# A decoder layer on one core: softmax normalised on POOL ahead of the transposes, in place of the spread and transposed reciprocals

## The chip, the cores and the metric

One core of a Trainium2 chip runs one program. The metric is the device time of an execution in microseconds; lower is better. Three runs of the kernel before took 1832.89, 1834.21 and 1837.18 us, median 1834.21.

## What is computed

32 sequences of 128 tokens, 512 wide, pass one decoder layer in fp32. Cut to what matters:

```python
x = x + attn(layernorm(x))              # 16 heads of 32, rotary, causal
x = x + xattn(layernorm(x), ctx)        # 32 heads of 16, axial rotary, ctx 128 x 256
x = x + ffn(layernorm(x))               # gate, up: 512 -> 1408, silu, down: 1408 -> 512
# both attentions, per head:
w = softmax(scores, axis=-1)            # rows: queries, columns: keys
ctx = w @ v                             # then @ Wo
```

The softmax is exp(s - max) divided by its row sum. The division can be made on the 128x128 probabilities of each head, or on the 32 or 16 output columns of that head.

## The kernel before

The program has two phases. The attention phase treats one sequence (128 tokens, one per partition) after the other; the FFN phase treats blocks of four sequences and is not touched by the change. Each engine has its own instruction stream, written out by hand in the function `turn` of its block, and streams wait for each other by semaphores. Nothing but the code's order sets the order of work.

A turn of the attention phase is a software pipeline over sequences. `turn(sq, cq, nx, nz, oq)` does for sequence sq its self-attention (unit "1": 16 heads), for cq = sq - 1 its cross attention in two halves ("2a" and "2b", 16 heads each), for nx the projections q1, k1, v1, for nz the first layernorm, and for oq = sq - 2 the last half of its cross attention and the output projection o2. The loop (`schedule`) has 27 such turns in a hardware loop and some more unrolled before and after it.

Each unit goes through the same steps with four PSUM banks S[0] to S[3], four heads to a bank:
- TensorE makes the scores (`scores1`, `scores2`) in all four banks.
- DVE takes the negated row maxima, a bank at a time (`row_maxima`, L831).
- ACT takes the exponentials into `prob` in SBUF, a head at a time, with the row sums accumulated (`exponentials`, L650).
- TensorE transposes the 16 heads' probabilities back into the same banks, a bank when it is ready (`transpose_prob`, through `transpose4`, L443).
- ACT copies banks 1 and 3 and DVE banks 0 and 2 to `probT` (`odd_copies` L657, `even_copies` L837). `collect` makes TensorE wait for all four before it writes the next scores into the banks.
- TensorE multiplies by v (`attend1` L497 into bank PC, `attend2` L507 into bank PB); the outcome is transposed: features on partitions.

While ACT takes exponentials, TensorE projects (`project`, L456: three passes over a high and a low part, since the fp32r operands hold less than fp32). The rotary embedding is made by DVE as two products (`rope`, L785 and L788), summed by POOL (`rope_sum`, L382), and transposed by TensorE.

The normalisation lies behind the attention. DVE takes the reciprocals of the row sums (L878 for unit 1, L937 for both halves of unit 2). POOL spreads each over its head's columns (`spread`, L388, to `rbc`, 128x512), TensorE transposes the spread tile by four transposes into bank TC, ACT copies it to SBUF (`rT1` L680, `rT2` L667), and DVE multiplies the attention's output by it twice, once rounded to `cn_h` and once in full to `cn` (`normalise_ctx`, L822 and L823). POOL takes `cn_l = cn - cn_h` (`ctx_low`, L401), and o1 and o2 are projected from the two parts.

The two layernorms share the pattern of `statistics` (DVE), `rough_rstd` (POOL, L378) and `normalise` (DVE: three small steps of one column, L768 to L771, then z, L773). POOL's stream also has `split_ctx` (L394, L397) and the sum x1B (L419). The rest of DVE's work in a turn: the residual sums x2 (L872) and x1A (L898), the reduction of a window of the FFN weights (L913), kT2 (L921, L922), kT1 (L928) and the low parts of z1T and z2T (L826).

Of the kernel before, what the change touches and what calls it, by code (L numbers as in the profile page):

```python
# [138 lines left out]
def attention_phase(nc, fp32, fp32r, ALU, ACT, AX, x, ctx_in, pos, consts,  # L139
                    wq1, wk1, wv1, wo1, wq2, wkv2, wo2, bout, x2_dram, shared_f, shared, ident, mhalf_c, ffn):  # L140
    es = ExitStack()
    with es:
# [42 lines left out]
        rsum1, rsum2 = sb("rsum1", [P, H1]), sb("rsum2", [P, H2])  # L185
        rinv1, rinv2 = sb("rinv1", [P, H1]), sb("rinv2", [P, H2])
        rbc1, rbc2 = sb("rbc1", [P, H1, DK1]), sb("rbc2", [P, H2, DK2])
        rT1, rT2 = sb("rT1", [P, D]), sb("rT2", [P, D])

        cn, cn_h, cn_l = sb("cn", [P, KT, P]), sb("cn_h", [P, KT, P], fp32r), sb("cn_l", [P, KT, P], fp32r)  # L190
# [13 lines left out]
        turns_sb, pos_sb = rT2[:, 0:B * 2 * HALF], rT2[:, B * 2 * HALF:B * 2 * HALF + 2 * B]  # L204
# [41 lines left out]
        rb_r = {n: sem(f"rinv{n}_spread") for n in (1, 2)}  # L246
        ri_d = {n: sem(f"rinv{n}T_done") for n in (1, 2)}
        riT_r = {n: sem(f"rinv{n}T_ready") for n in (1, 2)}
        cn_r = {n: sem(f"ctxn{n}_ready") for n in (1, 2)}
# [109 lines left out]
        def _(pool):  # L359
# [952 lines left out]
```

## Time and profile before

| | us |
|---|---|
| runs (3) | 1832.89 to 1837.18, median 1834.21 |
| profiled execution | 1831.93 |
| its span, first to last instruction | 1830.1 |
| busy: TensorE / DVE / ACT / POOL | 1699.3 / 1157.3 / 964.0 / 480.7 |
| mean granted TensorE clock | 0.977 |

The span is what the trace covers; the execution takes 1.8 us more. Each page and answer is of this one execution. A busy time is the sum of an engine's records; a group is all instructions of one line, operation and shape. The idle time before an instruction is given with what ended it. A line of `transpose4` or `project` is a helper's, so one tells its uses by the operands: `bank<-ident,prob` transposes probabilities, `bank<-ident,rbc` the spread reciprocals.

### The profile page before, as it was taken

Reading aid. Unit: us, or ns where it says so; the run is one execution under the profiler, and the core shown is the slowest. Engines: PE = TensorE matmul, PEld = TensorE weight load, DVE = VectorE, ACT = ScalarE, POOL = GpSimd, SP = SyncE. Lnnn points to the kernel's source line nnn. Section 1 sums busy time; section 2 is a strip of 40 time slices with the busy share of each in tenths; the row PEclk is TensorE's granted clock in tenths of the full one; section 3 lists DMA queues with packets and bytes.
Section 4 is the critical chain, followed back from the end, with each engine's and each line's share of the span. In section 5 each row is a group of like instructions: output and inputs, shape, how many; then the busy total and the mean of one; then the engine's idle time right before and its main releaser. Section 6 shows DMA issues by size and latency. Waiting matters only on the chain. (4 is left out here: it accounts for less than half of the span.)

```text
span 1830.1 us, 36507 instructions
## 1 busy us (share of the span) xinstructions
PE 1699.3 (93%) x12736; PEld 1376.3 (75%) x12736; DVE 1157.3 (63%) x2143; ACT 964.0 (53%) x3791; POOL 480.7 (26%) x470
## 2 busy tenths in 40 slices
PE   3799999999999999999999999997699999999997
PEld 2577777777777777777777777775478888888885
DVE  4677777777777777777777777765464343443432
ACT  4366666666666666666666666665342222222221
POOL 1233333333333333333333333332001110110111
PEclk8899999999999999999999999998699999999999
DMA  5010111001110011100101001020511101110110
GB/s 194 15 32 19 43 34 33 28 28 45 32 33 28 28 46 31 33 28 28 46 31 33 28 28 46 19 78 7 179 36 70 69 0 69 69 50 18 69 46 23
DMA packets 55095, 80.95 MB, mean 44 GB/s; under 512 B 4880, under 2 KB 25488, under 8 KB 55056
## 3 DMA queue, kind: packets, MB, share of 16 engines
q1 hardware_dynamic: 55056, 80.43, 13.5%
q8 instruction: 25, 0.41, 0.1%
q14 instruction: 14, 0.11, 0.0%
HBM read 63.63 MB, written 16.78 MB: 44 GB/s over the span
## 5 line engine op out<-in xcount | busy, mean ns | idle before, releaser
L650 ACT ACTIVATE prob<-bank,nmax 128x128 f32<-128x128 f32 x1536 | 537.4, 406 | 107.4 <-DVE nmax L831 107.4
L650 ACT ACTIVATION_READ_ACCUMULATOR prob<-bank,nmax 128x1 f32 x1536 | 378.4, 246 | 0.0
L831 DVE TENSOR_REDUCE nmax<-bank 128x4 f32<-128x512 f32 x384 | 240.9, 682 | 96.3 <-PE bank L478 71.0
L1107 PE MATMUL fbank<-shared,piece_hi 128*128 128x512 f32 x1152 | 280.3, 394 | 0.0
L1107 PEld LDWEIGHTS fbank<-shared,piece_hi 128*128 128x128 f32 x1152 | 215.8, 187 | 53.2
L382 POOL TENSOR_TENSOR rope_buf<-rope_buf 128x512 f32<-128x512 f32 x128 | 165.5, 1293 | 299.8 <-DVE rope_buf L788 299.4
L456 PE MATMUL bank<-shared,z1T_h 128*128 128x512 f32 x768 | 204.5, 409 | 5.1 <-DVE shared L945 3.8
L1259 DVE SCALAR_TENSOR_TENSOR h<-fbank,su_c,sil 128x512 f32<-128x512 f32 x88 | 66.0, 750 | 218.3 <-PE fbank L1107 218.2
L443 PE MATMUL bank<-ident,prob 128*128 128x128 f32 x1536 | 191.4, 277 | 11.0 <-ACT prob L650 11.0
L443 PEld LDWEIGHTS bank<-ident,prob 128*128 128x128 f32 x1536 | 174.4, 143 | 20.6 <-ACT prob L650 16.6
L657 ACT ACTIVATE probT<-bank 128x512 f32<-128x512 f32 x192 | 115.3, 600 | 130.4 <-PE bank L443 130.4
L456 PEld LDWEIGHTS bank<-shared,z1T_h 128*128 128x128 f32 x768 | 142.4, 192 | 47.4 <-issue 16.4
L1193 ACT ACTIVATE sil<-fbank,sg_c 128x512 f32<-128x512 f32 x88 | 60.4, 687 | 172.7 <-PE fbank L1107 171.9
L1199 ACT ACTIVATE h_h<-h 128x512 fp32r<-128x512 f32 x88 | 55.6, 632 | 177.1 <-DVE h L1259 177.1
L837 DVE COPY probT<-bank 128x512 f32<-128x512 f32 x192 | 126.3, 683 | 16.7 <-PE bank L443 14.8
L401 POOL TENSOR_TENSOR cn_l<-cn,cn_h 128x512 fp32r<-128x512 f32 x64 | 82.5, 1289 | 185.7 <-DVE cn L823 185.7
L388 POOL TENSOR_TENSOR rbc<-rinv,one_c 128x512 f32<-128x512 f32 x64 | 66.5, 1038 | 233.7 <-DVE rinv L937 182.3
L1122 PE MATMUL fbank<-piece_hi,h_h 128*128 128x512 f32 x288 | 115.3, 400 | 0.6 <-DVE h_l L1262 0.5
L1090 POOL TENSOR_TENSOR xr<-xr,ys 128x512 f32<-128x512 f32 x32 | 40.2, 1289 | 288.0 <-DVE ys L1279 288.0
L1122 PE MATMUL fbank<-piece_hi,h_l 128*128 128x512 f32 x288 | 113.6, 394 | 0.0
L456 PE MATMUL bank<-shared,z1T_l 128*128 128x512 f32 x384 | 105.0, 395 | 0.0
L1262 DVE TENSOR_TENSOR h_l<-h,h_h 128x512 fp32r<-128x512 f32 x88 | 62.8, 713 | 61.4 <-ACT h_h L1199 61.4
(156 smaller groups left out, 2925.7 us busy)
## 6 DMA issues: line engine op xcount, KB each, us to landing
xA<-in_x SPq DMA_DIRECT2D x32, 256.0 KB, 2.8
xB<-in_x SPq DMA_DIRECT2D x32, 256.0 KB, 2.8
x_scratch<-x SPq DMA_DIRECT2D x32, 256.0 KB, 2.0
shared_loaded<-x_scratch SPq DMA_DIRECT2D x8, 1024.0 KB, 7.7
xr<-x_scratch SPq DMA_DIRECT2D x8, 1024.0 KB, 5.6
out<-xr SPq DMA_DIRECT2D x8, 1024.0 KB, 4.3
cx<-in_ctx SPq DMA_DIRECT2D x32, 128.0 KB, 2.2
range_window<-in_wg SPq DMA_DIRECT2D x27, 112.0 KB, 2.0
```

The source lines that it names most:

```text
L382: pool.tensor_tensor(RA[n][:, :], RA[n][:, :], RB[n][:, :], ALU.add).then_inc(rot[n], 1)
L388: pool.tensor_tensor(tile[:, :, :], r[:, :].unsqueeze(2).to_broadcast([P, h, w]), one_c[:, :].unsqueeze(2).to_broadcast([P, h, w]), ALU.mu ...
L401: pool.tensor_tensor(cn_l[:, :, :], cn[:, :, :], cn_h[:, :, :], ALU.subtract).then_inc(cn_lo[n], 1)
L443: last = nc.tensor.transpose(dst[:, j * P:(j + 1) * P], src(j), ident[:, :])
L456: last = nc.tensor.matmul(dst[:, :], a[:, j, :], w[:, j, cols], start=(n == 0), stop=(n == 3 * k - 1))
L650: last = nc.scalar.activation(prob[:, c, i, :], S[c][:, i * P:(i + 1) * P], ACT.Exp, bias=nmax[:, c, i:i + 1], accum_out=rs[:, h:h + 1])
L657: nc.scalar.activation(probT[:, c, :, :].rearrange("p g t -> p (g t)"), S[c][:, :], ACT.Copy).then_inc(pTo_r[kind(u)], 1)
L831: nc.vector.tensor_reduce(out=nmax[:, c, :], in_=S[c][:, :].rearrange("p (g k) -> p g k", g=G), op=ALU.max, axis=AX, negate=True).then_inc ...
L837: nc.vector.tensor_copy(probT[:, c, :, :].rearrange("p g t -> p (g t)"), S[c][:, :]).then_inc(pTe_r[kind(u)], 1)
L1107: last = nc.tensor.matmul(dst[:, :], w[:, k, cols], z[:, k, :], start=(n == 0), stop=(n == len(passes) * KT - 1))
L1122: last = nc.tensor.matmul(DN[s][:, :], a[j % 2][:, tok], w[piece][:, j % 2, :], start=(j == 0 and n == 0), stop=(j == HT - 1 and n == len( ...
L1259: nc.vector.scalar_tensor_tensor(out=h[j % 2][:, :], in0=UP[j % 2][:, :], scalar=su_c[:, j:j + 1], in1=sil[j % 2][:, :], op0=ALU.mult, op1 ...
```

## The change

The probabilities are divided by their row sums before they are transposed.
- DVE takes reciprocals of two banks' sums at a time (`reciprocals`, six of 8 columns a turn), each when the exponentials of these two banks are done.
- POOL multiplies `prob` in SBUF, in place, a bank at a time, by the reciprocals broadcast over 128 keys (`normalise_prob`): 12 products of 128x512 a turn, in pairs.
- `transpose_prob` waits for these products (semaphore `prob1_normalised` or `prob2_normalised`) where it waited for the exponentials.
- `spread`, the transposes of `rbc`, the copies rT1 and rT2, the products `normalise_ctx` and POOL's `ctx_low` go, with their tiles and semaphores. ACT rounds the attention's output to `cn_h` (`ctx_high`, behind the exponentials of the next unit's bank 0), DVE takes `cn_l` from PSUM (`ctx_low`), and o1 and o2 wait for cn_l at their start.
- The transposes of 2b's banks 2 and 3 stand behind those of k1 and z1, and their copies accordingly.

Row sums and reciprocals share one tile for all units. The start-up scratch of the rotary tables moves from rT2 to x2.

```diff
@@ -182,12 +182,8 @@
 nmax = sb("nmax", [P, G, G])
-rsum1, rsum2 = sb("rsum1", [P, H1]), sb("rsum2", [P, H2])
-rinv1, rinv2 = sb("rinv1", [P, H1]), sb("rinv2", [P, H2])
-rbc1, rbc2 = sb("rbc1", [P, H1, DK1]), sb("rbc2", [P, H2, DK2])
-rT1, rT2 = sb("rT1", [P, D]), sb("rT2", [P, D])
-cn, cn_h, cn_l = sb("cn", [P, KT, P]), sb("cn_h", [P, KT, P], fp32r), sb("cn_l", [P, KT, P], fp32r)
+rsum, rinv = sb("rsum", [P, G, G]), sb("rinv", [P, G, G])
+cn_h, cn_l = sb("cn_h", [P, KT, P], fp32r), sb("cn_l", [P, KT, P], fp32r)
@@ -381,12 +374,12 @@
-def spread(n, q, r, tile, h, w):
-    wait(pool, ri_d[n], q)
-    pool.wait_ge(ri_r[n], q + 1)
-    pool.tensor_tensor(tile[:, :, :], r[:, :].unsqueeze(2).to_broadcast([P, h, w]),
-                       one_c[:, :].unsqueeze(2).to_broadcast([P, h, w]), ALU.mult).then_inc(rb_r[n], 1)
+def normalise_prob(u, q, half):
+    pool.wait_ge(ri_r[kind(u)], 2 * nth(u, q) + half + 1)
+    for c in (2 * half, 2 * half + 1):
+        pool.tensor_tensor(prob[:, c, :, :], prob[:, c, :, :], rinv[:, c, :].unsqueeze(2).to_broadcast([P, G, P]),
+                           ALU.mult).then_inc(pn_r[kind(u)], 1)
@@ -396,13 +389,9 @@
-def ctx_low(n, q):
-    pool.wait_ge(cn_r[n], q + 1)
-    pool.tensor_tensor(cn_l[:, :, :], cn[:, :, :], cn_h[:, :, :], ALU.subtract).then_inc(cn_lo[n], 1)
 def turn(sq, cq, nx, nz, oq):
-    if oq is not None:
-        ctx_low(2, oq)
+    if sq is not None:
+        normalise_prob("1", sq, 0)
@@ -411,25 +400,29 @@
     if sq is not None:
-        spread(1, sq, rinv1, rbc1, H1, DK1)
+        normalise_prob("1", sq, 1)
...
-    if sq is not None:
-        ctx_low(1, sq)
+    if cq is not None:
+        normalise_prob("2a", cq, 0)
     if nx is not None:
         rope_sum("q1", nx)
+    if cq is not None:
+        normalise_prob("2a", cq, 1)
...
+    if cq is not None:
+        normalise_prob("2b", cq, 0)
...
     if cq is not None:
-        spread(2, cq, rinv2, rbc2, H2, DK2)
+        normalise_prob("2b", cq, 1)
@@ -480,9 +473,9 @@
-def transpose_prob(u, q):
-    for c in range(G):
-        pe.wait_ge(p_r[kind(u)], G * nth(u, q) + c + 1)
+def transpose_prob(u, q, banks=range(G)):
+    for c in banks:
+        pe.wait_ge(pn_r[kind(u)], G * nth(u, q) + c + 1)
@@ -528,30 +521,19 @@
     if has_o:
-        pe.wait_ge(rb_r[2], oq + 1)
-        if has_c:
-            pe.wait_ge(zT_hi[2], cq + 1)
-            pe.wait_ge(zT_lo[2], cq + 1)
-        transpose4(TC, columns(rbc2[:, :, :].rearrange("p h d -> p (h d)"))).then_inc(ri_d[2], 1)
...
     if has_o:
-        pe.wait_ge(cn_r[2], oq + 1)
-        project(PB, cn_h, cn_l, "o2", KT, lo_ready=(cn_lo[2], oq + 1), fresh=is_first(oq)).then_inc(pj["o2"], 1)
-    if has_c:
-        if has_o:
-            pe.wait_ge(riT_r[2], oq + 1)
+        pe.wait_ge(cn_lo[2], oq + 1)
+        project(PB, cn_h, cn_l, "o2", KT, fresh=is_first(oq)).then_inc(pj["o2"], 1)
+    if has_c:
...
         transpose_prob("1", sq)
-        pe.wait_ge(rb_r[1], sq + 1)
-        if has_c:
-            pe.wait_ge(v2_r, cq + 1)
-        transpose4(TC, columns(rbc1[:, :, :].rearrange("p h d -> p (h d)"))).then_inc(ri_d[1], 1)
@@ -570,10 +552,11 @@
         pe.wait_ge(cxT_lo, sq + 1)
-        pe.wait_ge(riT_r[1], sq + 1)
+        if has_c:
+            pe.wait_ge(v2_r, cq + 1)
         project(TC, cxT_h, cxT_l, "kv2", CKT, slice(0, D), fresh=is_first(sq)).then_inc(pj["k2"], 1)
-        pe.wait_ge(cn_r[1], sq + 1)
-        project(PC, cn_h, cn_l, "o1", KT, lo_ready=(cn_lo[1], sq + 1), fresh=is_first(sq)).then_inc(pj["o1"], 1)
+        pe.wait_ge(cn_lo[1], sq + 1)
+        project(PC, cn_h, cn_l, "o1", KT, fresh=is_first(sq)).then_inc(pj["o1"], 1)
@@ -597,13 +580,15 @@
     if has_c:
-        transpose_prob("2b", cq)
+        transpose_prob("2b", cq, (0, 1))
...
         transpose_z1(nz)
+    if has_c:
+        transpose_prob("2b", cq, (2, 3))
@@ -639,20 +624,20 @@
-def exponentials(u, q):
-    rs = (rsum1, rsum2)[kind(u) - 1]
-    if u != "2b":
-        wait(act, ri_r[kind(u)], q)
-    for c in range(G):
+def exponentials(u, q, banks=range(G)):
+    for c in banks:
         act.wait_ge(nmax_r[kind(u)], G * nth(u, q) + c + 1)
         for i in range(G):
-            h = head(u, c, i)
             last = nc.scalar.activation(prob[:, c, i, :], S[c][:, i * P:(i + 1) * P], ACT.Exp,
-                                        bias=nmax[:, c, i:i + 1], accum_out=rs[:, h:h + 1])
+                                        bias=nmax[:, c, i:i + 1], accum_out=rsum[:, c, i:i + 1])
         last.then_inc(p_r[kind(u)], 1)
-def odd_copies(u, q):
-    for c in (1, 3):
+def ctx_high(n, q, src):
+    act.wait_ge(av_d[n], (q + 1) * n)
+    nc.scalar.activation(flat(cn_h), src[:, :], ACT.Copy).then_inc(cn_hi[n], 1)
+def odd_copies(u, q, banks=(1, 3)):
+    for c in banks:
@@ -662,11 +647,12 @@
             nc.scalar.activation(ffn["zT_h"][:, k, :], FZ[k][:, :], ACT.Copy).then_inc(f_zTh, 1)
+    if has_s:
+        exponentials("1", sq, (0,))
     if has_o:
-        act.wait_ge(ri_d[2], oq + 1)
-        nc.scalar.activation(rT2[:, :], TC[:, :], ACT.Copy).then_inc(riT_r[2], 1)
-    if has_s:
-        exponentials("1", sq)
+        ctx_high(2, oq, PB)
+    if has_s:
+        exponentials("1", sq, (1, 2, 3))
@@ -676,11 +662,13 @@
         odd_copies("1", sq)
-        act.wait_ge(ri_d[1], sq + 1)
-        nc.scalar.activation(rT1[:, :], TC[:, :], ACT.Copy).then_inc(riT_r[1], 1)
-    if has_c:
-        exponentials("2a", cq)
+    if has_c:
+        exponentials("2a", cq, (0,))
+    if has_s:
+        ctx_high(1, sq, PC)
+    if has_c:
+        exponentials("2a", cq, (1, 2, 3))
@@ -692,9 +680,11 @@
     if has_c:
-        odd_copies("2b", cq)
+        odd_copies("2b", cq, (1,))
     if nz is not None:
         z1T_high(nz)
+    if has_c:
+        odd_copies("2b", cq, (3,))
@@ -817,11 +807,6 @@
-def normalise_ctx(n, src, r):
-    nc.vector.tensor_tensor(flat(cn_h), src[:, :], r[:, :], ALU.mult).then_inc(cn_hi[n], 1)
-    nc.vector.tensor_tensor(flat(cn), src[:, :], r[:, :], ALU.mult).then_inc(cn_r[n], 1)
@@ -831,8 +816,17 @@
-def even_copies(u, q):
-    for c in (0, 2):
+def reciprocals(u, q, half):
+    c = slice(2 * half, 2 * half + 2)
+    dve.wait_ge(p_r[kind(u)], G * nth(u, q) + 2 * half + 2)
+    nc.vector.reciprocal(rinv[:, c, :], rsum[:, c, :]).then_inc(ri_r[kind(u)], 1)
+def ctx_low(n, q, src):
+    dve.wait_ge(cn_hi[n], q + 1)
+    low(cn_l, src[:, :], cn_h, cn_lo[n])
+def even_copies(u, q, banks=(0, 2)):
+    for c in banks:
@@ -855,9 +849,9 @@
     if has_o:
-        dve.wait_ge(riT_r[2], oq + 1)
-        dve.wait_ge(av_d[2], 2 * oq + 2)
-        normalise_ctx(2, PB, rT2)
+        ctx_low(2, oq, PB)
+    if has_s:
+        reciprocals("1", sq, 0)
@@ -865,6 +859,8 @@
         statistics(1, xA, nz)
+    if has_s:
+        reciprocals("1", sq, 1)
@@ -873,25 +869,23 @@
     if has_s:
-        dve.wait_ge(p_r[1], G * (sq + 1))
-        wait(dve, rb_r[1], sq)
-        nc.vector.reciprocal(rinv1[:, :], rsum1[:, :]).then_inc(ri_r[1], 1)
...
     if has_c:
-        row_maxima("2a", cq, (0, 1))
-    if has_s:
-        dve.wait_ge(riT_r[1], sq + 1)
-        dve.wait_ge(av_d[1], sq + 1)
-        normalise_ctx(1, PC, rT1)
-    if has_c:
-        row_maxima("2a", cq, (2, 3))
+        row_maxima("2a", cq, range(G))
+    if has_s:
+        ctx_low(1, sq, PC)
+    if has_c:
+        reciprocals("2a", cq, 0)
...
         rope("k2", sq, TC, DK2, *axial(sq), 1.0)
+    if has_c:
+        reciprocals("2a", cq, 1)
+    if has_s:
@@ -914,27 +908,29 @@
         ffn_normalise()
+    if has_c:
+        reciprocals("2b", cq, 0)
     if has_n:
         rope("k1", nx, PA, DK1, cos1, sin1, 1.0)
+    if has_c:
+        reciprocals("2b", cq, 1)
...
     if has_c:
-        even_copies("2b", cq)
+        even_copies("2b", cq, (0,))
...
         z1T_low(nz)
+    if has_c:
+        even_copies("2b", cq, (2,))
...
         low(z2T_l, TC[:, :], z2T_h, zT_lo[2])
-    if has_c:
-        dve.wait_ge(p_r[2], 2 * G * (cq + 1))
-        wait(dve, rb_r[2], cq)
-        nc.vector.reciprocal(rinv2[:, :], rsum2[:, :]).then_inc(ri_r[2], 1)
```

POOL's stream, first half of a turn (the unrolled one ahead of the loop; the loop's are alike). Before:

```order
L401 TENSOR_TENSOR cn_l<-cn,cn_h 128x512 [waits ctxn2_ready]
L382 TENSOR_TENSOR rope_buf<-rope_buf 128x512 [waits rope_q2_products]
L378 TENSOR_TENSOR r<-ve,mhalf 128x1 [waits var_eps1_ready]
L388 TENSOR_TENSOR rbc<-rinv,one_c 128x512 [waits rinv1_ready,rinv1T_done]
L394 TENSOR_TENSOR cxT_h<-cx,one_c 128x256 [waits proj_v2_done,ctx_loaded]
L397 TENSOR_TENSOR cxT_l<-cx,cxT_h 128x256 [waits ctxT_hi_ready]
L419 TENSOR_TENSOR x1B<-x1A,bout_b 128x512 [waits x2_ready,x1_ready]
```

The same stretch of the change:

```order
L381 TENSOR_TENSOR prob<-prob,rinv 128x512 [waits rinv1_ready]
L381 TENSOR_TENSOR prob<-prob,rinv 128x512
L375 TENSOR_TENSOR rope_buf<-rope_buf 128x512 [waits rope_q2_products]
L371 TENSOR_TENSOR r<-ve,mhalf 128x1 [waits var_eps1_ready]
L381 TENSOR_TENSOR prob<-prob,rinv 128x512 [waits rinv1_ready]
L381 TENSOR_TENSOR prob<-prob,rinv 128x512
L387 TENSOR_TENSOR cxT_h<-cx,one_c 128x256 [waits proj_v2_done,ctx_loaded]
L390 TENSOR_TENSOR cxT_l<-cx,cxT_h 128x256 [waits ctxT_hi_ready]
L408 TENSOR_TENSOR x1B<-x1A,bout_b 128x512 [waits x2_ready,x1_ready]
```

Two products stand ahead of rope q2 and the rough rstd, and two behind them. The second half of POOL's turn, before:

```order
L401 TENSOR_TENSOR cn_l<-cn,cn_h 128x512 [waits ctxn1_ready]
L382 TENSOR_TENSOR rope_buf<-rope_buf 128x512 [waits rope_q1_products]
L382 TENSOR_TENSOR rope_buf<-rope_buf 128x512 [waits rope_k2_products]
L378 TENSOR_TENSOR r<-ve,mhalf 128x1 [waits var_eps2_ready]
L382 TENSOR_TENSOR rope_buf<-rope_buf 128x512 [waits rope_k1_products]
L388 TENSOR_TENSOR rbc<-rinv,one_c 128x512 [waits rinv2_ready,rinv2T_done]
```

The same stretch of the change:

```order
L381 TENSOR_TENSOR prob<-prob,rinv 128x512 [waits rinv2_ready]
L381 TENSOR_TENSOR prob<-prob,rinv 128x512
L375 TENSOR_TENSOR rope_buf<-rope_buf 128x512 [waits rope_q1_products]
L381 TENSOR_TENSOR prob<-prob,rinv 128x512 [waits rinv2_ready]
L381 TENSOR_TENSOR prob<-prob,rinv 128x512
L375 TENSOR_TENSOR rope_buf<-rope_buf 128x512 [waits rope_k2_products]
L371 TENSOR_TENSOR r<-ve,mhalf 128x1 [waits var_eps2_ready]
L381 TENSOR_TENSOR prob<-prob,rinv 128x512 [waits rinv2_ready]
L381 TENSOR_TENSOR prob<-prob,rinv 128x512
L375 TENSOR_TENSOR rope_buf<-rope_buf 128x512 [waits rope_k1_products]
L381 TENSOR_TENSOR prob<-prob,rinv 128x512 [waits rinv2_ready]
L381 TENSOR_TENSOR prob<-prob,rinv 128x512
```

Each of the cross attention's halves has a rotary sum between its two pairs of products. On TensorE the end of a turn moves too (z is a layernorm's output). Before:

```order
L443 MATMUL bank<-ident,prob 128x128 [waits prob2_ready]
L443 MATMUL bank<-ident,prob 128x128 x3
L443 MATMUL bank<-ident,rope_buf 128x128 [waits rope_k1_ready]
L443 MATMUL bank<-ident,rope_buf 128x128 x3
L443 MATMUL bank<-ident,z 128x128 [waits z1_ready,v1_ready]
L443 MATMUL bank<-ident,z 128x128 x3
L443 MATMUL bank<-ident,z 128x128 [waits k2T_ready,z2_ready]
```

In the change:

```order
L436 MATMUL bank<-ident,rope_buf 128x128 [waits rope_k1_ready]
L436 MATMUL bank<-ident,rope_buf 128x128 x3
L436 MATMUL bank<-ident,z 128x128 [waits z1_ready,v1_ready]
L436 MATMUL bank<-ident,z 128x128 x3
L436 MATMUL bank<-ident,prob 128x128 [waits prob2_normalised]
L436 MATMUL bank<-ident,prob 128x128 x3
L436 MATMUL bank<-ident,prob 128x128 [waits prob2_normalised]
L436 MATMUL bank<-ident,prob 128x128 x3
L436 MATMUL bank<-ident,z 128x128 [waits k2T_ready,z2_ready]
```

The last two banks of 2b come behind k1 and z1, ahead of z2.

## Rows read from the trace of the kernel before

**Rows 1.** The page: busy us, share of the span and instructions of each engine
```profile
PE 1699.3 (93%) x12736; PEld 1376.3 (75%) x12736; DVE 1157.3 (63%) x2143; ACT 964.0 (53%) x3791; POOL 480.7 (26%) x470
```
**Rows 2.** Timeline of TensorE over one turn: start, duration, line, operation, [idle before <-releaser]
```profile
649.82 1.02 PE L463 MATMUL bank<-causal,ident_b 128*128 128x512 bf16 x4 [0.33 <-DVE kT L928]
...
652.69 0.63 PE L443 MATMUL bank<-ident,rbc 128*128 128x128 f32 x4 [0.75 <-POOL rbc L388]
...
661.73 1.91 PE L443 MATMUL bank<-ident,prob 128*128 128x128 f32 x16
...
664.38 1.15 PE L478 MATMUL bank<-kT,qT 32*128 32x256 f32 x16 [0.30 <-issue]
...
673.48 1.91 PE L443 MATMUL bank<-ident,prob 128*128 128x128 f32 x16
...
676.17 1.15 PE L478 MATMUL bank<-kT,qT 32*128 32x256 f32 x16 [0.34 <-ACT probT L657]
...
687.93 1.02 PE L463 MATMUL bank<-causal,ident_b 128*128 128x512 bf16 x4 [0.33 <-DVE kT L928]
```
**Rows 3.** TensorE's longest wait; scores1's first matmuls from 100 us on; the turn as a stretch
```profile
PE bank L443 <- POOL rbc L388: 28.5, 32, 3.6
L463 PE MATMUL bank<-causal,ident_b x120: 376/377/379, 116.5 to 1222.0; 128*128 128x512 bf16 x120
649.82:687.93 38.11, 36.40 (x329) 29.75 (x330) 28.37 (x55) 24.95 (x112) 13.42 (x13) 1.00 0.11 33
```
**Rows 4.** Timeline of POOL, DVE and ACT in the same turn
```profile
651.41 1.04 POOL L388 TENSOR_TENSOR rbc<-rinv,one_c 128x512 f32<-128x512 f32 x1 [5.24 <-DVE rinv L937]
652.01 2.48 DVE L831 TENSOR_REDUCE nmax<-bank 128x4 f32<-128x512 f32 x4 [0.75 <-PE bank L468]
658.85 1.29 POOL L382 TENSOR_TENSOR rope_buf<-rope_buf 128x512 f32<-128x512 f32 x1 [1.78 <-DVE rope_buf L788]
659.74 0.15 DVE L762 TENSOR_SCALAR ve<-mv 128x1 f32<-128x1 f32 x1
660.79 0.21 DVE L768 SCALAR_TENSOR_TENSOR nt<-r,ve 128x1 f32<-128x1 f32 x1
661.51 0.55 DVE L773 TENSOR_SCALAR z<-xA,mv,nt 128x512 f32<-128x512 f32 x1
661.97 0.25 DVE L878 RECIPROCAL rinv<-rsum 128x16 f32<-128x16 f32 x1
666.66 0.36 ACT L650 ACTIVATE prob<-bank,nmax 128x128 f32<-128x128 f32 x1
667.00 0.37 ACT L650 ACTIVATE prob<-bank,nmax 128x128 f32<-128x128 f32 x1
```
**Rows 5.** POOL's groups of the whole trace: count, busy us, mean ns of one, idle before
```profile
L382 POOL TENSOR_TENSOR rope_buf<-rope_buf 128x512 f32<-128x512 f32 x128 | 165.5, 1293 | 299.8 <-DVE rope_buf L788 299.4
L388 POOL TENSOR_TENSOR rbc<-rinv,one_c 128x512 f32<-128x512 f32 x64 | 66.5, 1038 | 233.7 <-DVE rinv L937 182.3 <-DVE rinv L878 51.4
L397 POOL TENSOR_TENSOR cxT_l<-cx,cxT_h 128x256 fp32r<-128x256 f32 x32 | 23.2, 726 | 2.5
L394 POOL TENSOR_TENSOR cxT_h<-cx,one_c 128x256 fp32r<-128x256 f32 x32 | 19.6, 613 | 0.7 <-DMA cx<-in_ctx 0.7
```
**Rows 6.** DVE beneath POOL in the FFN: timeline, and that line's ns (min/median/max)
```profile
1379.86 5.04 POOL L1090 TENSOR_TENSOR xr<-xr,ys 128x512 f32<-128x512 f32 x4 [30.11 <-DVE ys L1279]
1384.49 0.96 DVE L1262 TENSOR_TENSOR h_l<-h,h_h 128x512 fp32r<-128x512 f32 x1 [0.70 <-ACT h_h L1199]
L1262 DVE TENSOR_TENSOR h_l<-h,h_h x88: 691/691/975, 1320.8 to 1816.7; 128x512 fp32r<-128x512 f32 x88
```
**Rows 7.** The last attention turns: a stretch, and TensorE's scores 2a and last transposes there
```profile
1250.00:1300.00 50.00, 36.82 (x242) 27.30 (x242) 26.66 (x51) 24.16 (x95) 8.19 (x7) 0.70 0.02 6
1267.77 1.15 PE L478 MATMUL bank<-kT,qT 32*128 32x256 f32 x16 [0.80 <-ACT qT L676]
1275.51 1.11 PE L443 MATMUL bank<-ident,prob 128*128 128x128 f32 x4 [0.28 <-ACT prob L650]
```

More of the change, by code:

```diff
@@ L203, in attention_phase @@
         ang_s, ang_c = z2[:, 0:B * 2 * HALF], z2[:, B * 2 * HALF:2 * B * 2 * HALF]
-        turns_sb, pos_sb = rT2[:, 0:B * 2 * HALF], rT2[:, B * 2 * HALF:B * 2 * HALF + 2 * B]
+        turns_sb, pos_sb = x2[:, 0:B * 2 * HALF], x2[:, B * 2 * HALF:B * 2 * HALF + 2 * B]
         def whole(name):
@@ L245, in attention_phase @@
         ri_r = {n: sem(f"rinv{n}_ready") for n in (1, 2)}
[L246 to L249, printed above, removed]
+        pn_r = {n: sem(f"prob{n}_normalised") for n in (1, 2)}
         cn_hi = {n: sem(f"ctxn{n}_hi_ready") for n in (1, 2)}
```

## The prediction

> **What bounds the kernel now.** I read the page's engine shares and slices first. TensorE is busy 93% of the span, the next engine 63% [rows 1]. So I ask of every edit what it does to TensorE's queue. The timeline of TensorE over one turn of the attention loop gives three stages [rows 2]: A from scores1 (649.82) to the first scores2 (664.38), 14.56 us; B to the second scores2 (676.17), 11.79 us; C to the next scores1 (687.93), 11.76 us; together 38.11 us. Scores1 opens with four matmuls, and from 116.5 to 1222.0 us there are 120 of them, so 29 whole turns of that length [rows 3]. In a turn TensorE stands still only for fractions of a microsecond, the largest being its wait for the spread reciprocals, 28.5 us over 32 turns [rows 2, 3]. The turn taken as a stretch has the clock at 1.00, TensorE busy 36.40 us of the 38.11 and POOL 13.42 [rows 3]: POOL looks free. Each stage has one loop in it that runs through every engine: scores, row maxima (DVE), exponentials (ACT), transposes (TensorE), copies (ACT, DVE), next scores. The question is how long that loop gets once POOL stands in it. Below, all times are microseconds from the start of the stage.
>
> **Removed.** TensorE loses 8 transposes of spread reciprocals. At the start of A that is the wait of 0.75 and the four behind it, 0.56 at their pace. The other four, at the end of A, lie beside the copies for which the next scores wait anyway: from the start of bank 3's transposes (661.73 plus 3 x 0.44 = 663.04) to scores2 it is 1.34 in A, and 1.37 in B, with the four of q1 in between there [rows 2]. So they are worth nothing alone. ACT swaps two copies for two (rT for cn_h), DVE drops two of four products of 0.60 pace and gains four small reciprocals, about 0.2 each by the one of 0.25 for 16 columns [rows 4]; neither engine is late by it. No DMA is added, removed or moved. The o2 projection now waits for all of cn_l: maxima start at 2.2 (652.01) and go on at 0.60 [rows 4], exponentials of bank 0 run 2.9 to 4.3, the ACT copy to 4.9, the DVE difference to 5.65, and o2 starts at 6.1, without a wait. For o1 it is 4.65 against 6.37. POOL loses two cn_l, full operands like the sums' 1.29, and two spreads of 1.04 a turn [rows 5].
>
> **Added: twelve products of 128x512 a turn on POOL.** No row has this operation. The nearest are the spread, both operands broadcast, 1.038; the sums, two full operands, 1.293; and at half the width cxT_h, one full and one broadcast, 0.613 against cxT_l, two full, 0.726 [rows 5]. Two full operands thus cost 0.57 per 256 columns above 0.16 fixed; taking the same fixed part, one full and one broadcast give 0.16 + 2 x 0.453 = 1.07. I take 1.07, bounds 1.04 and 1.29. Four POOL sums of 1.29 in a row take 5.04 [rows 6], so successive ones overlap by 0.04, and the pace is 1.03. The Trainium skill, GPSIMD Engine Reference, Performance versus the Vector engine, puts a two-input body at about 2.6 cycles an element because both operands share a read port, however they are laid out; that would make it 1.29, as in the sums. The spread row speaks against it, since it too has two inputs; it is a rival below.
>
> Stage A. Exponentials start at 2.9 and go on at 0.343; behind the first four sits ACT's copy of cn_h, 0.5; the last sum is read 0.2 after its place: bank 1's sums are there at 2.9 + 8 x 0.343 + 0.5 + 0.2 = 6.4, all at 9.15 [rows 4]. The reciprocal is done at 6.62; rope q2 on DVE, now behind it, would have started at 6.43 and does at 6.57. POOL starts 6.70. Its queue is now product, product, rope q2, rough rstd, product, product: 6.70, 7.73, 8.76, 10.01, 10.51, 11.54 to 12.61. A POOL result reached TensorE 0.2 later (651.41 + 1.04 to 652.69) [rows 2, 4]. Bank 3's transposes begin at 12.82, where TensorE's own work would allow 12.0 (10.25 after v2, 0.44 for q2, 1.31 for three banks); add 1.34: 14.16.
> There is one more thing in A. DVE's z1 (0.55) waits for that rough rstd, and in DVE's queue the even copies stand behind it. DVE's h_l, two operands in SBUF, takes 0.691, but 0.96 when it starts at 1384.49 beneath a run of POOL sums that ends at 1384.90: it ended 0.55 after them [rows 6]. A one-column operation beneath a POOL sum was not held (ve at 659.74, 0.15 long, beneath 658.85 + 1.29) [rows 4]. The rough rstd is done at 10.56 and z1 comes 0.72 after the first small step, as in 660.79 to 661.51 [rows 4]: it would start at about 11.3, beneath a product. I take it that it waits till 11.58 and pushes the next product to 12.1: bank 3 then begins at 13.36, scores2 at 14.70, +0.14.
>
> Stage B. Exponentials from 1.9, with the cn_h copy behind bank 0; reciprocal 5.62. POOL: 5.70 product, 6.73 product, 7.76 rope q1, 9.01, 10.04 to 11.11. TensorE had its transposes at 9.10 (673.48) and bank 3 at 10.4; now bank 3 at 11.32, plus 1.37 is 12.69, +0.90.
>
> Stage C. The reciprocal comes behind the range reduction, 5.66. POOL: 5.75, 6.78, 7.81 rope k1, 9.06, 10.09 to 11.16. The order now puts k1's and z1's transposes between banks 1 and 2; they fill the wait, but bank 3 begins at 11.37 and the next scores at 12.71, +0.95, the kT waits covered. In B and C nothing covers the products' last part: the projections that hide the start of it end at 9.1 and 8.2, and behind them TensorE has only the transposes.
>
> Sum per turn: 0.14 + 0.90 + 0.95 = 1.99; times 29 = 58. The ends: the first turn's DVE chain, +0.5, and the second's rope q2 behind two products, +1.5 (estimates from the same steps); the last turn with scores1 about +1.1; in the last turn of cross attention transposes run at the pace of the exponentials, bank 3 at 1275.51 for scores at 1267.77 [rows 7], and would begin near +10.2 instead of +7.7, twice 2.45, less 1.3 for the spread's transposes and the shorter normalisation: +3.6. Together 7. The FFN is untouched. 1831.9 (profiled, 1.8 above its span) + 65 = **1897 us**; the median shown is 2.3 above the profiled run, about what a measurement of this kernel can't tell, which I set at 0.2% (3.7 us).
>
> **Rivals.**
> 1. No hold-up between DVE and POOL. z1 runs beneath the products, A is 14.16 (-0.40), a turn +1.45: 42 + 7, 1881. For: only one operation of the trace shows the hold-up, and it is no scalar one. Against: in z1's place DVE and POOL never overlap in this trace, so nothing shows that it would go free.
> 2. The one-column steps are held too. The first of z1's small steps reads two SBUF operands and asks at 10.6, just after a product began; it gets in at 11.6, the next at 12.8, z1 at 13.4, two even copies to 15.1, scores2 at 15.2: A +0.64, a turn +2.49, 72 + 7, 1911. The Trainium skill, SBUF — State Buffer, Who interferes with whom, states that a DVE instruction with two SBUF inputs, or in a 2-port mode, and a POOL instruction reading SBUF exclude each other for the whole instruction, whichever issues first. The h_l row agrees; no row here shows it for one column.
> 3. The product costs 1.29. Pace 1.25, twelve times 0.22 more: a turn about +4.1 to +4.6, with the ends 1959.
> 4. The other side: the products are covered. Sharing their place with the projections, POOL would have to be done before TensorE comes: then A is 12.0 + 1.34 = 13.34 (-1.22), B and C stay, a turn -1.22, about -35 in all and some 2 to 5 less at the ends, 1796. It decides on the product's price: all twelve lie on the loop, so against rival 1's +1.45 a turn the break-even is a pace of 1.03 - 1.45/12 = 0.91, an operation of 0.95. For: TensorE sheds 8 transposes and its longest wait, and DVE takes two operands of 512 columns in 0.69 [rows 6], so the arithmetic itself allows it. Against: no POOL row of 512 columns is under 1.04, even with nothing but broadcasts to read.
> 5. The clock falls. In the last attention turns it was 0.70 with TensorE busy 36.8 of 50 us [rows 7], which lies between the two levels of 1.2 and 2.4 GHz; in the loop it is 1.00 at 95% busy [rows 3]. With stalls near 1 us in each stage TensorE would be busy about 88%. If a tenth of its work ran at the low level, a turn would grow by over 3: above 1970.
>
> **How the numbers follow.** Forecast 0.37, rival 1 0.20, rival 2 0.18, rival 3 0.12, rival 4 0.10, rival 5 0.03. The range takes the first three with 15 us of error in the hand-worked waits below, and goes part of the way to rival 3: 1866 to 1945, 0.8. Of rival 4's 0.10, 0.08 is faster and 0.02 a gain or loss too small to tell; the rest, 0.90, is slower. The Trainium skill's rule of rival 2 would move the number by 14 us, not the sign.
>
> **What would show it.** A product row near 1.07 (1.29: rival 3; under 0.95: rival 4). POOL busy near 480.7 - 32 x 4.66 + 32 x 12.8 = 741 us. TensorE's waits headed by transposes released by POOL's products, about 0.9 us in B and 0.6 in C, in place of the 28.5 us for the spread. Stages of about 14.7, 12.7 and 12.7. z rows: 0.55 alone speaks for rival 1, 0.8 to 1.0 for the forecast, together with small steps above 0.2 for rival 2. I am wrong at the root if the stages B and C do not lengthen though the product takes 1.04 or more.

## The result, and the profile after

| | before | after |
|---|---|---|
| median of four runs each (us) | 1834.66 | 1896.85 |
| lowest to highest | 1832.89 to 1837.18 | 1896.36 to 1902.60 |
| profiled execution, its span | 1831.93, 1830.1 | 1902.60, 1900.7 |
| mean granted clock | 0.977 | 0.961 |

The ratio is 1.0347, interval 1.0329 to 1.0366: slower by 62 us. The forecast was 1897. The execution profiled is the longest of its four; the other three have spans of 1894.5 to 1895.1 and a clock of 0.964. The traces are compared as they are. Of the 70.5 us between them some 6 belong to that one execution of after, and 2.7 to the profiled one of before, which lies that much under its median.

The page of after, busy time of each engine and POOL's largest group, which answers to [rows 1] and [rows 5]:

```profile
PE 1712.4 (90%) x12448; PEld 1362.0 (72%) x12480; DVE 1187.2 (62%) x2207; ACT 966.5 (51%) x3791; POOL 720.9 (38%) x726
L381 POOL TENSOR_TENSOR prob<-prob,rinv 128x512 f32<-128x512 f32 x384 | 395.9, 1053 | 591.5 <-DVE rinv L822 591.3
```

POOL is still idle 62% of the span. TensorE has 288 instructions fewer, but of its span it is now idle 188.3 us (1900.7 less 1712.4), before 130.8. Its longest waits in after (us in total, times, longest), in place of the 28.5 us for the spread [rows 3]:

```profile
PE bank L436 <- POOL prob L381: 49.5, 80, 7.0
PE bank L471 <- DVE probT L831: 41.3, 31, 1.4
PE bank L456 <- ACT probT L642: 19.9, 26, 0.8
```

The first are the transposes behind the products, the second is scores2a at the end of stage A, the third the next scores1. Two turns of after, stage by stage (A, B, C, A, B, C): busy time of TensorE, its weight loads, DVE, ACT and POOL, then the granted clock, DMA share and GB/s:

```profile
649.36:663.94 14.58, 12.60 (x117) 9.88 (x118) 10.99 (x20) 8.66 (x39) 7.84 (x9) 1.00 0.05 18
663.94:677.30 13.36, 13.02 (x99) 10.44 (x99) 8.39 (x15) 7.54 (x36) 7.18 (x7) 0.87 0.00 0
677.30:689.96 12.66, 11.80 (x104) 9.51 (x105) 9.99 (x22) 8.76 (x38) 5.82 (x6) 1.00 0.27 79
689.96:704.54 14.58, 12.60 (x117) 9.86 (x118) 10.99 (x20) 8.71 (x39) 7.84 (x9) 1.00 0.05 18
704.54:716.94 12.40, 11.74 (x98) 9.31 (x98) 8.71 (x17) 7.50 (x36) 7.08 (x7) 1.00 0.00 0
716.94:729.64 12.70, 11.81 (x104) 9.52 (x105) 9.62 (x20) 8.79 (x38) 5.83 (x6) 1.00 0.27 79
```

Against 14.56, 11.79 and 11.76 of before, A has grown by 0.02, B by 0.61 or by about 1.55, C by 0.94. B comes in two lengths: in 15 of the 29 turns it has a granted clock of 0.87, and there it is 0.94 longer. The same matmuls took 13.02 us of TensorE in place of 11.74. These turns come two or three together, with two at full clock between.

**Where the 70.5 us of the two traces lie.** From the first scores1 with products (127.05, before 116.45) over 29 turns to 1289.49 (before 1221.33) it is 1162.4 against 1104.9: +57.5, of which the clock in B is 15 x 0.94 = 14. The stretch ahead of it grew by 10.6, the one behind it by 2.4 (611.2 against 608.8). Of the 10.6, 1.55 was there before any product had run: the z transposes ahead of the first scores1 begin at 43.84, in before at 42.29. Most of the rest is in the turns that still fill the pipeline. This stretch of after has the clock at 0.85, where 80 to 116.45 of before had 0.97:

```profile
80.00:127.05 47.05, 38.71 (x288) 30.87 (x288) 32.26 (x60) 25.94 (x113) 22.02 (x22) 0.85 0.05 15
```

**The end of stage A.** Timeline of POOL, DVE and TensorE in after, from rope q2's sum on (start, duration, line, operation, [idle before <-releaser]):

```profile
658.02 1.30 POOL L375 TENSOR_TENSOR rope_buf<-rope_buf 128x512 f32<-128x512 f32 x1
659.28 0.55 POOL L371 TENSOR_TENSOR r<-ve,mhalf 128x1 f32<-128x1 f32 x1
659.80 2.04 POOL L381 TENSOR_TENSOR prob<-prob,rinv 128x512 f32<-128x512 f32 x2
...
659.86 0.99 DVE L758 SCALAR_TENSOR_TENSOR nt<-r,ve 128x1 f32<-128x1 f32 x1 [0.46 <-POOL r L371]
660.88 0.15 DVE L760 TENSOR_SCALAR nt<-nt 128x1 f32<-128x1 f32 x1
661.07 0.78 DVE L761 TENSOR_TENSOR nt<-nt,r 128x1 f32<-128x1 f32 x1
661.98 0.71 DVE L763 TENSOR_SCALAR z<-xA,mv,nt 128x512 f32<-128x512 f32 x1
662.61 1.28 DVE L831 COPY probT<-bank 128x512 f32<-128x512 f32 x2
...
661.89 0.66 PE L436 MATMUL bank<-ident,prob 128*128 128x128 f32 x4 [0.34 <-POOL prob L381]
663.94 1.20 PE L471 MATMUL bank<-kT,qT 32*128 32x256 f32 x16 [1.40 <-DVE probT L831]
```

Two steps of one column last 0.99 and 0.78, the first 0.21 before [rows 4]. Each ends just after a product does (659.80 + 1.04 = 660.84; 661.84), so it was held while POOL worked. POOL was not: its pair of products took 2.04 without a gap. Behind the held steps stand z1 and the two even copies, and scores2a begins when the second copy is done, 1.40 after TensorE's last transposes.

### The profile page after: what moved, and what is told of

Read it like the earlier page. It is cut to its first block and busy times, and to the rows that moved or that the text cites. A ratio compares the mean times of both kernels' runs of the same rounds, so it can differ in the third digit from the quotient of the medians.

```text
span 1900.7 us, 36187 instructions
## 1 busy us (share of the span) xinstructions
PE 1712.4 (90%) x12448; PEld 1362.0 (72%) x12480; DVE 1187.2 (62%) x2207; ACT 966.5 (51%) x3791; POOL 720.9 (38%) x726
## 5 line engine op out<-in xcount | busy, mean ns | idle before, releaser
L381 POOL TENSOR_TENSOR prob<-prob,rinv 128x512 f32<-128x512 f32 x384 | 395.9, 1053 | 591.5 <-DVE rinv L822 591.3
L631 ACT ACTIVATION_READ_ACCUMULATOR prob<-bank,nmax 128x1 f32 x1536 | 383.0, 249 | 0.0
L436 PE MATMUL bank<-ident,prob 128*128 128x128 f32 x1536 | 221.7, 286 | 49.5 <-POOL prob L381 49.5
L449 PE MATMUL bank<-shared,z1T_h 128*128 128x512 f32 x768 | 210.2, 417 | 5.1 <-DVE shared L941 3.8
L449 PEld LDWEIGHTS bank<-shared,z1T_h 128*128 128x128 f32 x768 | 146.5, 198 | 51.3 <-issue 19.3
L471 PE MATMUL bank<-kT,qT 32*128 32x256 f32 x1024 | 81.7, 436 | 53.9 <-DVE probT L831 41.3
```

The lines of the kernel that those rows point to most:

```text
L381: pool.tensor_tensor(prob[:, c, :, :], prob[:, c, :, :], rinv[:, c, :].unsqueeze(2).to_broadcast([P, G, P]), ALU.mult).then_inc(pn_r[kind( ...
L436: last = nc.tensor.transpose(dst[:, j * P:(j + 1) * P], src(j), ident[:, :])
L449: last = nc.tensor.matmul(dst[:, :], a[:, j, :], w[:, j, cols], start=(n == 0), stop=(n == 3 * k - 1))
L471: last = nc.tensor.matmul(S[g][:, 2 * P * i:2 * P * (i + 1)], qT2[rows, j, :], kT2[rows, j, :, :].rearrange("p e t -> p (e t)"), start=Tru ...
L631: last = nc.scalar.activation(prob[:, c, i, :], S[c][:, i * P:(i + 1) * P], ACT.Exp, bias=nmax[:, c, i:i + 1], accum_out=rsum[:, c, i:i + 1])
```

## The experiments

Each kernel was timed beside runs of the kernel before on the same chip, whose medians were 1832.43 to 1833.28 us; the ratios are against these. After itself was timed in another set, in which before took 1834.66, so a difference from its 1896.85 carries some 2 us of doubt. Edits are against after, unless the text says otherwise.

### What the products cost as a whole

```diff
-for c in (2 * half, 2 * half + 1):
-    pool.tensor_tensor(prob[:, c, :, :], prob[:, c, :, :], rinv..., ALU.mult).then_inc(pn_r[kind(u)], 1)
...
-pe.wait_ge(pn_r[kind(u)], G * nth(u, q) + c + 1)
+pe.wait_ge(p_r[kind(u)], G * nth(u, q) + c + 1)
```

> The changed kernel without POOL's twelve products a turn; the transposes wait for the exponentials again, so the attention outputs stay unnormalised (this part of the computation is left out). Theory P (the products' time on the path is the loss): stages A, B, C of 13.4, 11.8, 11.8 us against 14.58, 12.4 or 13.3, 12.70 with them, about 1795 us in all. Rival O (the new order, the six reciprocals or the later cn_l cost time themselves): stages B or C stay above 12.3, and the time above 1834.

1812.31 us, ratio 0.988 (0.987 to 0.990); stages of e1, same columns as above:

```profile
608.90:622.10 13.20, 12.24 (x117) 9.92 (x118) 9.30 (x20) 8.54 (x38) 4.44 (x5) 1.00 0.05 20
622.10:633.90 11.80, 11.46 (x98) 9.38 (x98) 8.29 (x15) 7.50 (x36) 2.58 (x2) 1.00 0.00 0
633.90:646.35 12.45, 11.43 (x104) 9.58 (x104) 10.23 (x23) 8.96 (x38) 1.83 (x2) 1.00 0.26 80
```

The products cost 84.5 us (1896.85 less 1812.31), and what the change takes out, the spread and its transposes above all, is worth 1.36 in A. But I expected 1795 and missed by 17, because C did not fall back to 11.76. Its longest wait says why: scores1 waits for an even copy of DVE in 30 turns.

```profile
PE bank L453 <- DVE probT L828: 36.5, 30, 1.2
```

### The new order in stage C, without and with the products

The edit gives 2b's transposes and copies their old places, in one piece ahead of k1's and z1's; the first kernel also leaves out the products as above.

```diff
-transpose_prob("2b", cq, (0, 1))
+transpose_prob("2b", cq)
...
-transpose_prob("2b", cq, (2, 3))
...
-odd_copies("2b", cq, (1,))      # and even_copies (0,)
+odd_copies("2b", cq)            # and even_copies
...
-odd_copies("2b", cq, (3,))      # and even_copies (2,)
```

> Without products (left out as in e1), and with the four banks of 2b transposed and copied in one piece again, ahead of k1 and z1. Without products stage C was 12.45, not the 11.76 of before. Theory R (the new order causes it: DVE's copy of bank 2 comes behind kT1 and z1T's low part, and the next scores wait for it): stage C 11.76, total 1812 - 29 x 0.69 = 1792. Rival D (the reciprocals in DVE's queue or the ACT copy of cn_h cause it): stage C stays near 12.4, 1812.

1789.75 us (0.977, 0.975 to 0.978), C 11.77: as expected.

```profile
661.11:672.88 11.77, 11.44 (x104) 9.59 (x104) 9.50 (x22) 8.56 (x38) 1.83 (x2) 1.00 0.31 85
```

Without products the new order costs 0.69 a turn, since DVE's copy of bank 2 now stands behind kT1 and the low part of z1T, and scores1 waits for it. Without products and with the old order the rest of the change is worth 43 us against before.

> The changed kernel, products in place, with only the order of 2b's transposes and copies as before. Theory R2 (with products the order is worth having: k1's transposes and the kT copy no longer wait behind banks 2 and 3): stage C grows from 12.70 to about 13.2, total 1911. Rival: the order costs here too, as without products: stage C 12.7 or less, 1897 or less.

1914.93 us (1.046, 1.043 to 1.048); stages B and C of it:

```profile
625.68:639.00 13.32, 13.00 (x98) 10.30 (x99) 8.36 (x15) 7.49 (x36) 7.17 (x7) 0.87 0.00 0
639.00:652.02 13.02, 11.85 (x104) 9.55 (x105) 9.62 (x21) 8.23 (x37) 5.82 (x6) 1.00 0.27 77
```

With the products the order is worth 0.32 a turn in C, 9 of the 18 us. Another 6 are the clock in B, which is low here in 21 of 29 turns, not in 15; the other 3 were not placed. So the order belongs to the change, though by itself it is a loss. In the old order the products cost 125 us (1914.93 less 1789.75), in the new one 84.5. This confirms the prediction's point that k1's and z1's transposes fill the wait.

### The clock in stage B

TensorE has nothing to do at the end of A but to wait for a copy. If that pause is what drops the clock in the next stage, four useless transposes of the identity in it must end the drop, and cost nothing.

```diff
 transpose_prob("1", sq)
+if has_c:
+    pe.wait_ge(v2_r, cq + 1)
+for _ in range(1):            # 3 in the second kernel
+    transpose4(TC, lambda j: ident[:, :])
```

> The changed kernel with four transposes of the identity into the free bank TC behind unit 1's transposes, where four transposes of the spread reciprocals stood before. They lie in TensorE's wait of 1.40 us. Theory C (the idle end of stage A makes the clock fall in some turns, 13.34 instead of 12.40 in stage B in about half of them): stage B is 12.40 in all turns, the granted clock 1.00 there, about 29 x 0.45 = 13 us less, 1884. Rival N (four are not enough, or the drop has another cause): 1897, stage B as mixed as before. Rival L (they delay something): stage A longer than 14.58.

1884.21 us (1.028, 1.026 to 1.029), 12.6 less than after. A turn of it, A, B, C:

```profile
640.15:654.71 14.56, 13.02 (x122) 10.31 (x123) 10.99 (x20) 8.64 (x39) 7.83 (x9) 1.00 0.05 18
654.71:667.09 12.38, 11.73 (x98) 9.30 (x99) 8.70 (x17) 7.48 (x36) 7.07 (x7) 1.00 0.00 0
667.09:679.78 12.69, 11.80 (x104) 9.54 (x104) 9.61 (x20) 8.77 (x38) 5.82 (x6) 1.00 0.26 79
```

A is as long as before with 0.42 us more of TensorE in it, and no B has the 0.87.

> The same with twelve transposes of the identity, 1.3 us, which fill the wait of 1.40 us almost whole. Theory C: stage B 12.40 in all turns, 1884, stage A 14.6. If four were too few and the cause is TensorE's idle time, only this one reaches it. If the drop has another cause, 1897 or more.

1885.06 us (1.029, 1.027 to 1.030): three times the filler fills the pause to 0.08, gains nothing more and costs nothing, with A still 14.56. TensorE is not what ends A.

The traces of e1 and e8 bear the pause out from the other side. There TensorE pauses 0.73 ahead of scores2a in the 30 turns behind the first, and B has its clock of 1.00 in each. In the first alone, while the pipeline fills, the pause is 2.20, and B has 0.87. Timeline of TensorE in e1, and the stage behind:

```profile
96.51 1.40 PE L468 MATMUL bank<-kT,qT 32*128 32x256 f32 x16 [2.20 <-DVE probT L828]
96.51:109.88 13.37, 13.03 (x98) 10.27 (x99) 8.53 (x15) 7.54 (x36) 2.58 (x2) 0.87 0.06 12
```

### The held-up small steps

The first and the third small step of `normalise` become a form that takes its further operands as per-partition scalars:

```diff
-link(nc.vector.scalar_tensor_tensor(out=t[:, 1:2], in0=r0[n][:, :], scalar=ve[n][:, :], in1=r0[n][:, :],
-                                    op0=ALU.mult, op1=ALU.mult))
+link(nc.vector.tensor_scalar(t[:, 1:2], r0[n][:, :], ve[n][:, :], r0[n][:, :], ALU.mult, ALU.mult))
...
-link(nc.vector.tensor_tensor(t[:, 3:4], t[:, 2:3], r0[n][:, :], ALU.mult))
+link(nc.vector.tensor_scalar(t[:, 3:4], t[:, 2:3], r0[n][:, :], None, ALU.mult))
```

> The changed kernel with layernorm's small steps that read two SBUF tensors written as tensor-scalar operations with pointer scalars (same arithmetic). Theory H (DVE's steps with two SBUF tensors are held until POOL's product ends, 0.99 and 0.78 us instead of 0.21 and 0.16, and the even copies behind z1 are what scores 2a waits for): the steps take 0.15 to 0.21 each, scores 2a no longer waits for DVE, stage A falls to between 14.0 and 14.5, and with a shorter wait the clock holds: 1870 to 1885. Rival S (pointer scalars or z itself are held alike): steps or z still 0.7 to 1.0 us, stage A 14.58, 1897.

1871.85 us (1.021, 1.019 to 1.023), A 14.00. TensorE's pause ahead of scores2a is 0.83 for 1.40, and no B has a lower clock; C is 12.80 for 12.70. Timeline of POOL, TensorE and DVE at the end of its stage A:

```profile
604.44 2.04 POOL L381 TENSOR_TENSOR prob<-prob,rinv 128x512 f32<-128x512 f32 x2
606.44 0.80 POOL L387 TENSOR_TENSOR cxT_h<-cx,one_c 128x256 fp32r<-128x256 f32 x1
...
608.02 1.15 PE L471 MATMUL bank<-kT,qT 32*128 32x256 f32 x16 [0.83 <-DVE probT L830]
...
604.51 0.27 DVE L758 TENSOR_SCALAR nt<-r,ve 128x1 f32<-128x1 f32 x1 [0.45 <-POOL r L371]
605.01 0.21 DVE L760 TENSOR_SCALAR nt<-nt,r 128x1 f32<-128x1 f32 x1
605.35 1.42 DVE L762 TENSOR_SCALAR z<-xA,mv,nt 128x512 f32<-128x512 f32 x1
```

The steps run beneath the products: the first takes 0.27 here whether POOL works or not. z1 now asks at 605.35, within the first product, and ends at 606.77: it gets in only behind both, not between them, and then holds cxT_h (0.80, else 0.61). So a one-column step is held or not by its form. At 512 columns `tensor_tensor` was held (h_l, [rows 6]) and `tensor_scalar` too, as z1 here.

The other way out is to put z1 behind the even copies:

```diff
-if nz is not None:
-    normalise(1, xA, z1, nz)
 if has_s:
     even_copies("1", sq)
+if nz is not None:
+    normalise(1, xA, z1, nz)
```

> The changed kernel with DVE's small steps and z1 moved behind unit 1's even copies; z1's transposes are only in stage C. Theory H2 (the hold-ups cost because the even copies stand behind them; the steps may stay held): scores 2a is released by ACT's copy of bank 3, 1.34 us after the start of its transposes at 12.5: stage A 13.9, no long idle stretch of TensorE, stage B 12.4 in all turns, 1863 us. Rival: z1 gets late for its transposes or its steps collide with stage B's row maxima: stage B or C longer by 0.3 or more, 1872 or above.

1867.93 us (1.019, 1.018 to 1.021), and no lower clock in B:

```profile
630.87:644.76 13.89, 12.60 (x117) 9.87 (x118) 9.43 (x19) 8.71 (x39) 7.15 (x9) 1.00 0.05 19
644.76:657.33 12.57, 11.88 (x98) 9.36 (x99) 10.06 (x18) 7.51 (x36) 7.71 (x7) 1.00 0.00 0
657.33:670.01 12.68, 11.80 (x104) 9.51 (x104) 9.60 (x20) 8.79 (x38) 5.82 (x6) 1.00 0.27 79
```

A gains 0.69, B loses 0.17 to the z1 that now stands ahead of its row maxima. It is the best kernel here with the whole change in it, and still 35 us slower than before. So the hold-up and the clock explain 29 of the 62 us. Of the 35 that are left, 30 are the stages: against before A is 0.67 shorter, B 0.78 and C 0.92 longer, 1.03 a turn.

### The break-even

The products take half the keys only (`prob[:, c, :, 0:P // 2]`), so that their number, places and waits stay and only their duration falls.

> The changed kernel with each of POOL's twelve products over the first 64 of 128 keys only (the other half of the probabilities stays unnormalised, left out). A product should take 0.61 us, as cxT_h of 256 columns did. Theory B (there is a break-even: below about 0.95 us the products end before TensorE's projections do, and more cover brings nothing): all of the products' cost goes, stages 13.2, 11.8, 12.45 as without products, about 1812 us. Rival Q (cost in proportion to POOL's work): half of the 84 us goes, 1855.

1813.41 us (0.990, 0.988 to 0.991), with the stages of e1. These, and POOL's group:

```profile
607.14:620.33 13.19, 12.25 (x117) 9.92 (x118) 9.63 (x20) 8.54 (x38) 6.34 (x9) 1.00 0.05 20
620.33:632.13 11.80, 11.46 (x98) 9.38 (x99) 8.29 (x15) 7.51 (x36) 5.32 (x7) 1.00 0.00 0
632.13:644.59 12.46, 11.43 (x104) 9.58 (x105) 10.25 (x23) 8.96 (x38) 4.14 (x6) 1.00 0.27 80
L381 POOL TENSOR_TENSOR prob<-prob,rinv 128x256 f32<-128x256 f32 x384 | 231.8, 625 | 632.6 <-DVE rinv L822 632.2
```

At 0.63 us a product all twelve are hidden; at 1.04 they cost 84 us. What a chain of four products adds depends on when the last of them is ready against the moment at which TensorE would come for it, 10.4 us in B [rows 2]. Where between 0.63 and 1.04 the cost sets in, no run shows. An estimate for B: at a pace of 1.00 it is 0.60 longer than here (12.40 less 11.80), with four products in a row, so it would set in at a pace of about 0.85.

### The kernel before with its wait mended

What the change really removed was one wait, that for the spread of unit 2, and eight transposes (1.36 in A). In the kernel before, that spread is late because DVE takes unit 2's reciprocals last in a turn, behind kT2, though the exponentials are done far earlier. The edit, against before, moves the block up:

```diff
 rope("k1", nx, PA, DK1, cos1, sin1, 1.0)
+if has_c:
+    dve.wait_ge(p_r[2], 2 * G * (cq + 1))
+    wait(dve, rb_r[2], cq)
+    nc.vector.reciprocal(rinv2[:, :], rsum2[:, :]).then_inc(ri_r[2], 1)
...
-if has_c:
-    dve.wait_ge(p_r[2], 2 * G * (cq + 1))
-    wait(dve, rb_r[2], cq)
-    nc.vector.reciprocal(rinv2[:, :], rsum2[:, :]).then_inc(ri_r[2], 1)
```

> The kernel before, with DVE's reciprocals of unit 2 moved from the end of its turn to the place ahead of kT2, where it idles 1.67 us. The spread is then done long before TensorE comes to its transposes. If the wait for the spread (28.5 us over 32 turns, 0.75 us a turn) is the part of the old normalisation that costs time, stage A falls from 14.56 to 13.8 and the total by 29 x 0.75 = 22 us to 1812, below both kernels. Rival: the wait passes to the next one (the maxima or the copies behind it), stage A stays above 14.3 and the total above 1825.

1812.53 us, ratio 0.989 (0.987 to 0.991): 21 us less than before, and 84 less than after. A turn of it, A, B, C:

```profile
640.50:654.27 13.77, 13.26 (x125) 10.78 (x126) 10.34 (x21) 8.99 (x40) 5.05 (x6) 1.00 0.05 19
654.27:666.07 11.80, 11.46 (x98) 9.38 (x99) 8.55 (x14) 7.44 (x36) 5.48 (x5) 1.00 0.00 0
666.07:677.82 11.75, 11.43 (x104) 9.58 (x104) 9.57 (x21) 8.56 (x38) 2.89 (x3) 1.00 0.30 85
```

A is 0.79 shorter than before, the wait; the 0.57 from there to e1's 13.20 is what the rest of the removal adds, the transposes above all. The head of TensorE's list of waits is now kT's, at 16.8 us:

```profile
PE bank L463 <- DVE kT L932: 16.8, 30, 1.0
```

## Why the prediction was right, and where not

**Right: the reading that POOL's free time was no cover.** The twelve products stand in a loop that runs through every engine, and in B and C nothing else covers the last pair. e1 and e6 show it from both sides.

**Right: the price.** 1.07 was forecast at a pace of 1.03; the median is 1.042 and pairs take 2.04, a pace of 1.00. POOL's busy time came to 720.9 for 741. Rival 3 is out: two full operands take 1.29, with one broadcast it is 1.04. From e6's median of 0.615 to 1.042, 256 columns more cost 0.43 us, with two full operands 0.57 [rows 5]. The Trainium skill's figure for two operands (GPSIMD Engine Reference, Performance versus the Vector engine) fits the sums and not this product; the page says nothing of broadcast operands. Rival 4 is out by the price: e6, at 0.63, is on its side of the break-even of 0.95. But a turn gained 0.66 there (38.11 less 37.45) and not the 1.22 that I gave it, since I had counted the new order as free.

**Stage B, mis-sized and missing a case.** At a clock of 1.00 it came out at 12.40 for 12.69: the pace saved 0.17 at the end of the second pair (10.94 for 11.11), and the transposes followed it by 0.06, not the 0.2 that I had put in. The wait for the product ahead of the last bank, given as 0.9 in B and 0.6 in C, shows as 0.34 in both. Rival 5 happened, but not as I priced it: I gave it 0.03 and over 3 us in every turn; it came as 0.94 in one stage of 15 turns. So the sum lacks 14 us. I looked for it in TensorE's busy share over a turn, and what decided was one pause at the end of A.

**Stage C, right by two errors.** 12.70 for 12.71; the last transposes began at 11.09 (728.03 less 716.94), not 11.37, but scores1 came 1.6 behind them, not 1.34.

**Stage A, right in length and wrong in its step.** I had the one-column steps run free, z1 held, and the next product pushed to 12.1, so that the last bank's transposes would begin at 13.36. That is the step that failed: they began at 12.53 (661.89 less 649.36). The row from which I took it that the steps run free, ve in [rows 4], reads one operand from SBUF; the step that was held reads two. The small steps are held (0.99 and 0.78), z1 hardly (0.71 for 0.55), the pair of products is not parted, and the stage ends on DVE's second copy. This is rival 2's mechanism; it had A at 15.2, since I let a waiting DVE step and a product take turns. The Trainium skill's rule (SBUF — State Buffer, Who interferes with whom) holds in these rows for the two-input steps of one column too; which of its forms are free, e4 shows. So 14.58 for 14.70 is no proof of my chain.

**The ends.** Forecast +7, measured +13: the filling turns cost more than the 2 I gave them, 10.6 (1.55 of it ahead of any product), again with a low clock, the tail less, 2.4 for nearly 5.

**The sum.** Without the clock, 29 turns grew by 57.5 - 14 = 43.4, for 58 forecast: a turn by 1.50, not 1.99. The clock put 14 on top, the ends 6 more than forecast. The forecast hit the median within 1 us, and missed the profiled execution by 6; its terms were off by some 15 to 20 us in each direction. That they cancel is luck.

**Expectations of the experiments.** e1 missed by 17 because I had counted the new order as free; e8 and e9, made for it, came out as expected. It stays open why the clock drops in 15 turns and not in the other 14, of which 13 have a pause as long; no run was made for that.

## What to carry to other kernels

An engine that is 26% busy offers cover only where its work does not stand in the chain between two scores; ask of each added operation when its input is complete and when its reader comes, and compute the duration at which it turns from free to costly before making the edit. When a change is to remove a wait, look first at why its releaser is late: moving one reciprocal ahead in DVE's stream gained 21 us, with none of the restructuring. After a stage gets longer, read the granted clock of the stage behind it, and try a few useless matmuls in the pause before judging the change.

## What the hardware did that I had not expected

**A short pause cost clock in the next stage.** In after TensorE pauses 1.40 us at the end of A in 28 of 29 turns, with 0.34 before it, and in 15 of these the next stage has a granted clock of 0.87, between the levels of 1.2 and 2.4 GHz; 0.42 us of identity transposes in the pause, which left 0.96 of it, or a pause of 0.83 (e4) or 0.73 (e7), kept 1.00 in every one of the 29. The Trainium skill (TensorE: Matmul & The Clock Gate, Why this matters for your kernels) warns of longer idle gaps than these; here the measurement decides.

**Who waits when DVE and POOL meet in SBUF depends on the form and on what is queued.** Within a pair of POOL products DVE did not get in (z1, 1.42). At the start of after, beside the splitting of the weights, both grew. Timeline of POOL and DVE there:

```profile
50.77 6.02 POOL L381 TENSOR_TENSOR prob<-prob,rinv 128x512 f32<-128x512 f32 x2 [7.73 <-DVE rinv L822]
...
50.61 2.24 DVE L941 TENSOR_TENSOR w_o_lo<-w_o_lo_loaded,w_o_hi 128x2048 fp32r<-128x2048 f32 x1
52.76 3.13 DVE L941 TENSOR_TENSOR w_kv_lo<-w_kv_lo_loaded,w_kv_hi 128x2048 fp32r<-128x2048 f32 x1
```

Two products of 1.04 took 6.02 us together, and the second weight split 3.13 for 2.24. So here POOL was held too, and the two engines seem to have taken turns by whole instructions. How much of the start's growth this makes was not separated.
